# Counting patch ends with small digit products and reordering the start of a fused attention kernel

## The reference

```python
attn = jnp.einsum('bhnd,bhmd->bhnm', q * scale, k)      # k, v: context rows, then own rows
attn = jax.nn.softmax(attn, axis=-1)
out = jnp.einsum('bhnm,bhmd->bhnd', attn, v)
```

```python
bidx = jnp.cumsum(patch_lens, axis=1) - 1
boundary_mask = boundary_mask.at[jnp.arange(bsz)[:, None], bidx].set(1)
plug = jnp.clip(jnp.cumsum(boundary_mask, axis=1) - 1, 0, plen - 1)
depool_out = depool[jnp.arange(bsz)[:, None], plug]
```

## Time and profile before

| | |
|---|---|
| three runs | 1152.93, 1152.98, 1156.45 us |
| median | 1152.98 us |
| the profiled execution | 1152.34 us, of which its span is 1150.5 us |
| PE busy | 1062.2 us (92%) |
| DVE busy | 937.9 us (82%) |
| ACT busy | 815.3 us (71%) |
| POOL busy | 693.4 us (60%) |

### The profile page before, as it was taken

How to read it: one execution, slowest core, us unless ns; L and a number is a source line. 1 busy time by engine, 2 the same in 40 slices (tenths; PEclk the granted TensorE clock), 3 DMA queues, 4 the chain that set the end, 5 groups by cost and what they waited for, 6 DMA issues and landing times.

```text
span 1150.5 us, 33448 instructions
## 1 busy us (share of the span) xinstructions
PE 1062.2 (92%) x8458; PEld 711.5 (62%) x8458; DVE 937.9 (82%) x2332; ACT 815.3 (71%) x1730; POOL 693.4 (60%) x1255
## 2 busy tenths in 40 slices
PE   5789999999999999999999999999999959988885
PEld 3356666666666666666666666666665537777773
DVE  5867878878888788888888887887777857999997
ACT  3167777777777777777777777777776648888773
POOL 6455555666655666666666666555555127778776
PEclk9799999999999999999999999999999988999997
DMA  4433333333334333343334344334333101222222
GB/s 140 118 88 103 102 106 104 99 99 99 99 100 113 101 103 105 104 106 103 106 105 107 102 105 105 104 101 107 93 97 83 47 27 44 81 80 80 87 89 91
DMA packets 158680, 110.18 MB, mean 96 GB/s; under 512 B 17154, under 2 KB 154788, under 8 KB 158628
## 3 DMA queue, kind: packets, MB, share of 16 engines
q1 hardware_dynamic: 158356, 109.30, 35.1%
q10 hardware_dynamic: 272, 0.26, 0.1%
HBM read 30.30 MB, written 16.29 MB: 40 GB/s over the span
## 4 chain that ended last, share of the span: by engine, by line
PE 61%; DVE 13%; issue 8%; SPq 6%; POOL 5%; DMA 4%; ACT 1%; DVEq 1%; POOLq 0%; ACTq 0%
PE pv_ps L676 14%; PE ms_ps L661 13%; PE st_ps L651 12%; PE misc L699 9%; PE misc L707 3%; SPq L424 3%; SPq L422 3%; DVE neg L897 3%; DMA q<-negT 2%; PE misc L702 2%; PE aux L723 2%; PE aux L728 1%; DVE am L1281 1%; DVE xs L1270 1%; PE misc L691 1%
## 5 line engine op out<-in xcount | busy, mean ns | idle before, releaser
L897 DVE TENSOR_REDUCE neg<-ms_ps 128x1 f32<-128x376 f32 x1024 | 527.4, 544 | 165.5 <-PE ms_ps L661 158.0
L991 ACT ACTIVATE probs<-st_ps 128x512 f32<-128x512 f32 x768 | 428.7, 598 | 34.9 <-PE st_ps L651 30.2
L661 PE MATMUL ms_ps<-k,q 96*128 96x376 bf16 x1024 | 334.6, 328 | 23.1 <-DVE neg L897 18.6
L651 PE MATMUL st_ps<-q,k 99*128 99x256 bf16 x1536 | 294.6, 273 | 6.4 <-DMA q<-negT 5.7
L651 PEld LDWEIGHTS st_ps<-q,k 99*128 99x128 bf16 x1536 | 136.5, 98 | 127.1 <-issue 39.6
L676 PE MATMUL pv_ps<-probs,v 128*32 128x256 f32 (+1 forms) x3072 | 193.9, 385 | 0.0
L699 PE MATMUL misc<-xnT,wqkvT 128*128 128x256 f32 x512 | 155.6, 388 | 2.6 <-ACT xnT L1017 1.9
L661 PEld LDWEIGHTS ms_ps<-k,q 96*128 96x128 bf16 x1024 | 98.6, 96 | 93.0 <-DVE neg L897 59.1
L513 POOL TENSOR_SCALAR negp<-neg 128x16 bf16<-128x16 f32 x64 | 13.1, 205 | 196.8 <-DVE neg L897 196.8
L676 PEld LDWEIGHTS pv_ps<-probs,v 128*32 128x32 f32 (+1 forms) x3072 | 87.3, 110 | 69.5 <-issue 23.4
L699 PEld LDWEIGHTS misc<-xnT,wqkvT 128*128 128x128 f32 x512 | 92.9, 196 | 7.8 <-ACT xnT L1017 2.8
(11 more groups left out here) (188 smaller groups left out, 1834.5 us busy)
## 6 DMA issues: line engine op xcount, KB each, us to landing
k<-parts SPq DMA_DIRECT2D x384, 94.0 KB, 2.7
q<-parts SPq DMA_DIRECT2D x384, 64.0 KB, 2.4
out_dram<-xn SPq DMA_DIRECT2D x32, 256.0 KB, 2.2
xs<-in_x SPq DMA_DIRECT2D x31, 256.0 KB, 2.8
cx<-in_ctx SPq DMA_DIRECT2D x32, 240.0 KB, 2.9
recurrence_input<-u_in SPq DMA_DIRECT2D x32, 120.0 KB, 2.3
plug<-plugs SPq DMA_DIRECT2D x32, 120.0 KB, 3.5
powers<-gath SPq DMA_DIRECT2D x32, 120.0 KB, 1.9
```

What stands on the lines that cost most here:

```text
L651: mm = pe.matmul(st_ps[u % SR][:, j * S:(j + 1) * S], k6[0:KM, r, h, k * P:(k + 1) * P], q6[0:KM, r, h, :], start=True, stop=True)
L661: pe.matmul(ms_ps[t][:, 0:KEYS], q6[0:KR, r, h % HU, t * P:(t + 1) * P], k6[0:KR, r, h % HU, 0:KEYS], start=True, stop=True).then_inc(s_ms, 1)
L897: dve.tensor_reduce(neg[:, m, t, h % HU:h % HU + 1], ms_ps[t][:, 0:KEYS], AX.X, ALU.max, negate=True).then_inc(s_red, 1)
L991: act.activation(probs[:, u % PR, :], st_ps[u % SR][:, :], ACT.Exp).then_inc(s_exp, 1)
```

## The change

- The lengths are fetched earlier (own semaphore `d_lens`).
- DVE's `setup` splits half 0 of batch 0, and POOL half 1.
- ACT issues five of the six key transfers of that first stack (`first_keys`, between iterations -2 and -1); SP issues the six query transfers and one key transfer.
- The ends become two base-16 digits. DVE makes one-hot rows of both digits for all batches in two comparisons (120 x 32 x 16 each, one bf16 row per digit). In step 5 of iteration -1, ahead of the first maxima product, PE makes 32 products of 16 x 16, one per batch: entry (h, l) counts the ends at place 16 h + l. ACT copies them out in step 6, SP takes them through DRAM into rows of 256, and DVE caps them as before. The 32 comparisons, the selector and its 32 products go.
- On POOL, in iteration -1, the split of the first maxima stands ahead of both splits of batch 1. On SP, in iteration -1, the counts, the context and `neg0` stand ahead of both stacks of batch 1.

```diff
 setup (DVE):
-                f = qk[:, 1, :]
+                f = qk[:, 0, :]
...
+                dve.wait_ge(s_set_pe, 3)
+                dve.tensor_scalar(ends_i[0:NP, 0, :], pv_ps[0:NP, 0:NB], -1.0, 2.0 * S - 1.0, ALU.max, ALU.min).then_inc(s_ends, 1)
+                dve.wait_ge(s_ends, 5)
+                dve.tensor_scalar(ends_i[0:NP, 1, :], ends_i[0:NP, 0, :], 4, None, ALU.arith_shift_right).then_inc(s_ends, 1)
+                dve.tensor_scalar(ends_i[0:NP, 2, :], ends_i[0:NP, 0, :], HEX - 1, None, ALU.bitwise_and).then_inc(s_ends, 1)
+                for digit in range(2):
+                    dve.wait_ge(s_ends, 6 + digit)
+                    dve.tensor_tensor(digits[0:NP, digit, :, :], ends_i[0:NP, 1 + digit, :].unsqueeze(2).broadcast_to([NP, NB, HEX]),
+                                      iota_i[0:NP, 0:HEX].unsqueeze(1).broadcast_to([NP, NB, HEX]), ALU.is_equal).then_inc(s_hots, 1)
                 dve.wait_ge(s_set_pe, 2)
-                dve.tensor_copy(wprojT[:, :, :], pv_ps[:, :].rearrange("p (k c) -> p k c", c=C)).then_inc(s_wproj, 1)
...
+                dve.tensor_copy(wprojT[:, :, :], st_ps[0][:, :].rearrange("p (k c) -> p k c", c=C)).then_inc(s_wproj, 1)
 body (DVE):
-                    if isinstance(b, int) and b == -1 and HOT0 <= u < HS - 1:
-                        for j in range((u - HOT0) * HOTS, (u - HOT0 + 1) * HOTS):
-                            dve.tensor_scalar(hots[0:NP, j, :], iota_s[0:NP, :], endsT[0:NP, j:j + 1], None,
-                                              ALU.is_equal).then_inc(s_hots, 1)
 body (PE):
-                        pe.wait_ge(s_hots, (u - HOT0) * HOTS)
...
+                    if isinstance(b, int) and b == -1 and u == AT_COUNTS:
+                        pe.wait_ge(s_hots, 2)
+                        for j in range(NB):
+                            mm = pe.matmul(pv_ps[0:HEX, j * HEX:(j + 1) * HEX], digits[0:NP, 0, j, :], digits[0:NP, 1, j, :],
+                                           start=True, stop=True)
+                        mm.then_inc(s_counts, 1)
 ACT:
+            def first_keys():
+                for part, steps in ((0, 1), (1, 3)):
+                    act.wait_ge(s_split0, steps)
+                    for slot in range(SLOTS):
+                        if K_PART[slot] == part:
+                            act.dma_start(k6[slot * D:slot * D + D, 0, :, 0:KEYS], parts[:, 0, part, S:FC]).then_inc(d_stack[0], 16)
...
+                    if isinstance(b, int) and b == -1 and u == AT_COUNTS + 1:
+                        act.wait_ge(s_counts, 1)
+                        act.copy(counts_sb[:, :, :], pv_ps[0:HEX, :].rearrange("p (b l) -> p b l", l=HEX)).then_inc(s_counts, 1)
...
-            iterations(act, body, {-1: staged})
+            iterations(act, body, {-2: first_keys, -1: staged})
 body (POOL):
+                if isinstance(b, int) and b == -1:
+                    split_neg(0, 0, b)
                 if live(b + 2):
-                    split(b, 0, i, par, opp)
+                    split(b, 0 if live(b + 1) else 1, i, par, opp)
 body (SP), ahead of the stack of half 0 of b + 2:
+                if isinstance(b, int) and b == -1:
+                    sp.wait_ge(s_counts, 2)
+                    sp.dma_start(count_dram.rearrange("b (h l) -> h b l", l=HEX), counts_sb[:, :, :]).then_inc(d_counts, 16)
+                    load_cx()
+                    sp.wait_ge(d_counts, 16)
+                    sp.dma_start(steps[:, 0, :], count_dram).then_inc(d_counts, 16)
+                    rows_0()
```

More of the change, by code:

```diff
@@ L47, in flamingo_two_layers @@
     SLOTS = 6
+    HEX = 16
     KR = SLOTS * D
@@ L73, in flamingo_two_layers @@
     powers_dram = nc.dram_tensor("powers", (NB, NP, S), F32, kind="Internal").ap()
+    count_dram = nc.dram_tensor("counts", (NB, S), F32, kind="Internal").ap()
     plug_dram = nc.dram_tensor("plugs", (NB, S), F32, kind="Internal").ap()
@@ L303, in splits @@
         def splits(B, m):
-            return 0 if isinstance(B, int) and B * 2 + m == 0 else (B * 2 + m - 1) * 4
+            return (B * 2 + m - 1) * 4
         def live(b):
@@ L371, in flamingo_two_layers @@
         N_IDENT = 4
-        N_IOTA = 17
-        N_SEL = 20
-        N_V = 22
-        N_CONST = 24
-        N_W = 5
+        N_IOTA = 15
+        N_CONST = 21
+        N_W = 4
         N_ROW = 3
@@ L414, in stack @@
                 for part, steps in ((0, 1), (1, 3), (2, 4)):
-                    if isinstance(B, int) and B == 0 and m == 1:
+                    first = isinstance(B, int) and B * 2 + m == 0
+                    if first:
                         sp.wait_ge(s_split0, steps)
@@ L422, in stack @@
                             sp.dma_start(q6[rows, r, :, :], parts[:, m, part, 0:S]).then_inc(d_stack[r], 16)
-                        if K_PART[slot] == part:
+                        if K_PART[slot] == part and not (first and part < 2):
                             sp.dma_start(k6[rows, r, :, 0:KEYS], parts[:, m, part, S:FC]).then_inc(d_stack[r], 16)
@@ L453, in body @@
                     sp.dma_start(powers_dram[b - 1], gath[0:NP, opp, :]).then_inc(d_pow[opp], 16)
-                if live(b + 3) and live(b + 1):
-                    own_wait(sp, s_vcx, b + 2)
-                    sp.wait_ge(s_u, (b + 1) * 4 + 3)
-                    sp.dma_start(cx[0:NP, opp, :], ctx_2048[b + 3]).then_inc(d_cx[opp], 16)
-                if live(b + 1):
-                    own_wait_taken(sp, b, "neg0")
-                    sp.dma_start(q6[KR:KM, 2 * opp, :, :], negT[:, 0, :]).then_inc(d_neg[2 * opp], 16)
+                if live(b + 3) and live(b):
+                    load_cx()
+                if live(b + 1) and live(b):
+                    rows_0()
                 if live(b + 2):
@@ L754, in body @@
                     all_scores(others)
-                    if isinstance(b, int) and b == -1 and u >= HOT0 + 1:
-                        if u == HOT0 + 1:
-                            pe.wait_ge(s_wproj, 1)
-                            pe.wait_ge(s_const, N_SEL)
-                        pe.wait_ge(s_hots, (u - HOT0) * HOTS)
-                        for j in range((u - HOT0 - 1) * HOTS, (u - HOT0) * HOTS):
-                            mm = pe.matmul(pv_ps[0:NB, 0:S], sel[0:NP, NB - j:2 * NB - j], hots[0:NP, j, :],
-                                           start=(j == 0), stop=(j == NB - 1), skip_group_check=True)
-                        if u == HS - 1:
-                            mm.then_inc(s_bound, 1)
+                    if isinstance(b, int) and b == -1 and u == AT_COUNTS:
[4 more added lines that the diff above has]
+                        mm.then_inc(s_counts, 1)
                     if isinstance(b, int) and b == NB - 1:
@@ L813, in setup @@
                 dve.wait_ge(s_split0, 2)
[L814 removed]
+                dve.tensor_scalar(parts[:, 0, 1, :], f, 1.0, 0.0, ALU.mult, ALU.add).then_inc(s_split0, 1)
                 dve.wait_ge(s_split0, 3)
[L816 removed]
+                dve.tensor_tensor(parts[:, 0, 2, :], f, parts[:, 0, 1, :], ALU.subtract).then_inc(s_split0, 1)
```

61 lines of the change are left out of this document (31 added, 30 removed).

## The result

The changed kernel takes 1148.63 us (median of 20 runs, 1142.97 to 1153.21) beside 1152.76 for the kernel before (20 runs, 1149.84 to 1156.83). The ratio is 0.9959 with a 95% interval of [0.9946, 0.9972], which is 4.7 us less (3.2 to 6.2). Forecast were 4.5 less.

What follows compares the result with a forecast made beforehand. TensorE bounds the loop, so the start decides: batch 0 begins 7.0 us earlier, 2.5 go back to SP's queue, and 1152.98 - 4.5 = 1148.5. Its own range is 1146.8 to 1150.8; with rivals, 1145.8 to 1151.8.

Steps and rivals of the forecast that it cites:

- 16th reduction to the rows' DMA: Ahead of batch 0: from 40.9 through GpSimd, TensorE and ScalarE to SP's issue of the first maxima rows at about 43.9.
- first to second rows: SP's queue from the first maxima rows at 43.9, past 24 stack transfers, to the second maxima rows at 60.2.
- from there to batch 1's first rows: SP's queue in batch 0's stage after the second maxima rows: unchanged, 14.06 us, batch 1's rows issued at 74.3.
- The queue ahead of the second rows: On SP: 24 transfers at 0.64, 15.4 us, hold the second maxima rows, ready by 58.5, until 60.2.
- The counts: TensorE, right ahead of the first maxima product: 32 products of 16 columns take 2.4 us, bounds 1.0 to 4.0.
- The stack of half 0: Batch 0's first stack: last issue 23.5, landed 2.56 later at 26.1 instead of 29.1, 3.0 earlier.
- This, not the stack, is what ends last: TensorE's q products of batch 1, delayed by ScalarE's issues, end at 28.1 to 29.0; 3.0 won turns into 1.0.
- the way from the first product to the 16th reduction: VectorE ahead of batch 0: 5.5 to the eighth reduction plus 4.6 for nine more, 10.1 at the lower clock.
- The first stack of batch 1: In batch 0's stage: lands at 54.4 where TensorE would want it at 53.6, 0.8 lost.
- The full gain: Rival, chance 0.08: SP has slack and all 7.0 us won at batch 0's start stay, 1146.0.
- ScalarE and the counts push the first product: Rival, chance 0.17: first maxima product at 32.5 to 34, gain only 1 to 3, say 1151.
- The slower clock in batch 0's stage: Rival, chance 0.07: TensorE's clock falls at 62.4 and stays down, batch 1 starts at 84.7, about 1158.

Runs made afterwards that it cites:

- the longer queue: Changed kernel with four extra 32 KB transfers on SP ahead of batch 1's first maxima rows: 1150.52 us, ratio to the kernel before 0.9986.
- both controls: The changed kernel, unchanged, profiled a second and a third time: 1144.07 and 1147.75 us.
- ScalarE's second rows: Changed kernel, but ScalarE instead of SP issues batch 0's second maxima rows: 1147.34 us, ratio to the kernel before 0.9952.
- the counting alone: Changed kernel with SP issuing batch 0's whole first stack, batch -1 ordered as before, GpSimd splitting half 0 and VectorE half 1: 1149.82 us, ratio 0.9986.
- SP's issues: Changed kernel, but SP issues all twelve transfers of batch 0's first stack: 1148.93 us, ratio to the kernel before 0.9966.
- the old order and ScalarE's issues: Changed kernel, but in iteration -1 GpSimd's split and SP's stack of batch 1's half 0 precede the first maxima and their rows: 1148.21 us, ratio 0.9951.
- SP's issues in the old order: Changed kernel with SP issuing all of the first stack and iteration -1 ordered as in the kernel before: 1149.30 us, ratio 0.9963.
- the plug's: As SP's issues in the old order, but the plugs' wait and read back follow six transfers of batch 2's stack: 1148.10 us, ratio 0.9965.
- the new order alone: Kernel before, comparisons kept, with only iteration -1 reordered so the first maxima and their rows precede batch 1's splits and stacks: 1153.59 us, ratio 1.0011.

## Why the prediction was right, and where its sizes were off

**The bound and the way of the gain were as read.** Reductions free of the comparisons, then a stage of batch 0 that gives part back: the rows of both show it. Three steps were met within 0.7: 16th reduction to the rows' DMA (3.0, measured 2.8 to 2.9), first to second rows (16.3, measured 16.5 to 16.9), and from there to batch 1's first rows (14.1, measured 13.4 to 14.0). That the start of batch 0 wins more than is kept held as well: 7.0 and 4.5 forecast, 10.2 and 6.7 measured.

**The queue ahead of the second rows held in some executions only.** The prediction said that it was wrong if the second maxima rows don't wait for SP. Five profiles run the same program up to there. In two they waited (1.0 in the first profile of after, 1.6 with the longer queue). In three (both controls, 0.1 each, and ScalarE's second rows) they were ready only when the 24 transfers had ended. In the two, TensorE's clock was 1.00 from batch 0's start to these rows and its wait for the first stack of batch 1 was 1.61 and 1.39; in the three the clock was 0.88 and the wait 2.24 to 2.45. So there a slower stage and not the queue gave back part of the gain, by about the same amount. What the clock answers to is open.

**The counts were 2.5 times too dear.** 2.4 (1.0 to 4.0) were put down for 32 products; they took 0.96, 30 ns each, less than the lower bound. The nearest row, value products with 256 moving columns at 62.5 ns a pair, was the wrong one to be near to. The Trainium skill's rule (page "TensorE: Matmul & The Clock Gate", section "Part 2: What happens when you issue a matmul"), one column a cycle, gave an estimate that the prediction put at 0.5; the 512 columns are 0.43 us at 1.2 GHz and 0.21 at 2.4. The same section also gives a floor of about 25 ns for products of 1 to 64 columns, by which 32 are an estimate of 0.8 us; the prediction didn't use it. The trace, 30 ns each, agrees with the floor nearly, and a stretch at half clock shows that columns aren't what bounds it: the same 32 take 0.96 there too, in the kernel with the counting alone (by stretch, with the granted clock third from the end):

```profile
26.43:28.43 2.00, 0.96 (x32) 0.86 (x32) 1.85 (x6) 0.52 (x2) 1.94 (x2) 0.50 0.58 141
```

**The stack of half 0 was sized too early, and that moved little.** Landed at 26.1 was forecast, 7.8 after the split; it was 11.0 to 11.7, no earlier than before (10.8). The step that failed is "landed 2.56 after the last issue", from a row with one queue at work. With two, landings take 4.8 to 6.8; with one, in the experiment with SP's issues, the last took 3.5, and the stack landed at 11.2, although by VectorE's split its first transfer was issued 0.6 sooner than before. "This, not the stack, is what ends last" failed with it: the first product starts 0.05 to 0.15 after the stack's last landing in all three profiles, and the q products and the counts end just then (idle ahead of the product 0.57, 0.0 and 0.0). Stack too early and counts too dear cancel nearly, which is luck: the product comes 0.7 to 1.3 earlier than the 12.5 forecast.

**The reductions ran faster than at the clock of before.** 10.1 was taken for the way from the first product to the 16th reduction, "if the clock is the lower one as it was". It was 9.9 in one profile and 8.6 in the controls. The six microseconds from the first product on, in the second profile of after:

```profile
28.53:34.53 6.00, 5.03 (x22) 2.18 (x20) 5.40 (x11) 2.56 (x6) 3.39 (x8) 1.00 1.20 123
```

in the first:

```profile
30.80:36.80 6.00, 5.39 (x18) 3.11 (x18) 4.28 (x9) 0.89 (x3) 2.30 (x5) 0.72 1.21 120
```

and with SP's issues alone:

```profile
28.36:34.36 6.00, 5.67 (x16) 3.38 (x16) 3.62 (x8) 0.00 (x0) 2.86 (x6) 0.52 0.63 108
```

The second profile ran these at the full 2.4 GHz, the others part or nearly all of the time at 1.2. What TensorE did before: in five profiles (both controls of after, and the experiments with the old order and ScalarE's issues, with ScalarE's second rows and with the longer queue) it went from the counts to the first maxima product without a gap (0.06 at most), and the clock in the six microseconds was 0.98 to 1.00. In the others it had idled, by 0.57 (first profile of after), 1.37 and 1.45 (SP's issues in the old order, and the plug's), 1.89 (SP's issues), 2.56 (the counting alone) or 3.5 and more (before, and the new order alone); there the clock was 0.50 to 0.72. With the counts, the 16th reduction came 8.5 to 8.7 after the product in the five and 9.9 to 10.6 in the rest. So ScalarE's issues may bring 1.3 us in a way that nobody put into a sum: they delay the q products until these run straight into the maxima. That was found in the profiles afterwards. No experiment moved the gap alone, so it is what goes together in these profiles and not a cause that was shown. It fits 1.2 of the 1.7 us between the two kernels of the old order (54.7 and 56.4), and 1.3 of the 2 by which the first profile of after lies behind its controls.

**What queues on SP past the rows.** The first stack of batch 1 was to land with 0.8 lost to TensorE; the wait measured 1.61, 2.42 and 2.45. Here, too, landings are longer: the median of the 24 in the row is 3.4 to 3.8 in the profiles of after and 3.0 to 3.1 for the twelve of the old order, where it was 2.6 before. The length of the row is the smaller part of that, since the kernel before with nothing but the new order has 24 in a row as well and 2.6. The larger part holds for every stack of the loop. The page of the kernel before (its part on DMA issues, median us to landing last):

```profile
k<-parts SPq DMA_DIRECT2D x384, 94.0 KB, 2.7
q<-parts SPq DMA_DIRECT2D x384, 64.0 KB, 2.4
```

and of the changed kernel:

```profile
k<-parts SPq DMA_DIRECT2D x379, 94.0 KB, 3.2
q<-parts SPq DMA_DIRECT2D x384, 64.0 KB, 3.0
```

All four profiles with the comparisons show 2.7 and 2.4, all ten with the digits 3.2 and 3.0, also those in which SP alone issues. So the change made every stack transfer land 0.5 us later, which no term of the prediction has. The code of these transfers is the same; that tiles stand elsewhere since `iota_s`, `endsT` and `sel` went is a guess that no run tests.

**What was forecast as 4.5 and what the 4.7 are made of.** The sum stopped at batch 1's start, and two things lie behind it. Batch 1's stage is 27.5 to 27.8 us in after and 28.3 to 29.2 in before (in two of the three with a drop of the clock): 1.2 more won. From the start of batch 3 to that of batch 31 it takes 769.4 to 770.2 in after and 768.6 to 769.3 in before: 0.8 given back. Why these iterations, whose code is unchanged, are 0.03 us longer each stays open; the later landings go together with it (all ten profiles with the digits are above 769.3, all four with the comparisons below). By the means of three spans each 6.7 are won in all (1144.99 for 1151.65), by the timed runs 4.7 (3.2 to 6.2). The row phase alone (from the attention phase's last projection product on) takes 214.4 to 217.3 us from one of these six profiles to the next, in no order by kernel, and the start 17 to 21, so three profiles can't say more. The forecast's total agrees with the timed runs, while at batch 1 it was 2.0 too late (58.5 for a mean of 56.5, or 2.2 too little gained). The 2.0 between 6.7 and 4.7 need no cause in the kernel: the three profiled executions of after are on average 1.9 us below the median of its 20 runs (1146.78 for 1148.63), those of before 0.7 above theirs (1153.45 for 1152.76). So the forecast's total was met, but terms that were off by 1 to 4 us cancelled on the way to it, and that is partly luck. Some bounds are also 0.1 to 0.2 off their own sums (4.5 less 2.2 is 2.3, not 2.2), which moves nothing.

**The rivals.** The full gain: no, 3.5 were given back. ScalarE and the counts push the first product: it comes 0.4 to 0.9 later than before, not 3.4, and with SP's issues alone it comes no earlier, so the landing of the stack is enough to explain it. The slower clock in batch 0's stage: there in two of the three profiles, but small. In the first profile of after the stage ran at 1.00 with waits of 1.61 and 1.99; in the second, after its wait of 2.42, it shows 0.94 and TensorE busy for 1.3 us more (25.54 for 24.21):

```profile
42.54:73.15 30.61, 25.54 (x194) 14.68 (x192) 19.74 (x47) 20.05 (x44) 22.13 (x33) 0.94 0.52 124
```

That is far from the 15 us of lower clock from which it would have decided.

No version is shown to beat the changed kernel. The old order with ScalarE's issues begins batch 1 earliest (54.7) and has the lowest span but one, but its interval [0.9933, 0.9969] holds the 0.9959.

## What to carry to other kernels

Before an operation is moved ahead in a queue, count what then lies between it and the next urgent one: here the rows gained 3 us and the next ones left 1 us later than in the old order, because two stacks came to stand between them instead of one. A second issuing engine is worth its issue time only where issuing is what ends last; look at the landing times with both queues at work first. Before a difference is put down to an edit, look whether it arises ahead of it: two kernels with the same program up to a mark differed by 2 us there. And compare starts by marks from a common event, since the absolute times of two executions of one program differ by up to 4 us.

## What the runs showed of the hardware

- With SP and ScalarE both issuing, the median landing of stack transfers rose from 3.1 to 3.3 us to 4.5 to 6.8, and the packets' times added up from 46.9% to 83.5%, at about the same bytes per second (119 and 114 GB/s in 14 us). The twelve transfers were issued 2.4 us earlier and landed no earlier (11.0 to 11.7 for 11.2). SP's own transfers are slowed with it.
- Comparisons of 120 x 256 bf16 on VectorE took 0.27 to 0.28 us each while GpSimd was idle, and up to 1.4 while it ran (in the three profiles of before); four in a row took 0.86 and up to 2.55, and 3.04 beside the splits of batch 1 in the new order.
- 32 products with 16 moving columns each, back to back, took 0.96 us at either clock, 30 ns each.
- A wait of 2.0 to 2.4 us was followed by a clock of 0.94 over the stage (before, batch 1; second profile of after, batch 0) and also by 1.00 (after 2.44 us, in the kernel with the longer queue). What decides it is open.
- The stack transfers of the whole loop, with the same code, landed in 2.7 and 2.4 us (k and q) in all four profiles with the comparisons and in 3.2 and 3.0 in all ten with the digits. The cause is open.
- Two comparisons of 120 x 512 whole numbers with a bf16 result took 2.3 to 2.5 us together on VectorE, always beside work of GpSimd: about 1.2 each, or 0.69 and 1.87 (the second profile of after). What they take alone no run shows.
